# Second expert layer in three 16-bit products on 128-column tiles, its turns taken expert by expert, and the gating as one product a group with a GpSimd addition

## The reference, cut to what matters

```
x = x + windowed_attention(layernorm(x))          # 7x7 windows, 12 heads of 8, shifted by 3 or 4
t = x as tokens
scores = layernorm(t) @ gate_w + gate_b           # 4 experts
probs = softmax(scores);  keep the best 2, divide by their sum
h[e] = gelu(layernorm(t) @ w1[e] + b1[e])         # 96 -> 384, exact gelu
y[e] = h[e] @ w2[e] + b2[e]                       # 384 -> 96: the second expert layer
out = t + sum over e of gate[e] * y[e]
```

## Time and profile before

| | us |
|---|---|
| median of three runs | 7177.02 |
| lowest and highest | 7176.89, 7177.97 |
| the profiled execution | 7177.81 |
| its span, first to last instruction | 7176.0 |
| PE busy | 6927.8 (97%) |
| DVE busy | 5426.9 (76%) |
| ACT busy | 4147.0 (58%) |
| POOL busy | 1515.2 (21%) |
| mean granted TensorE clock | 0.997 of full |

### The profile page before, as it was taken

How to read it: one execution, slowest core, us unless ns; L and a number is a source line. 1 busy time by engine, 2 the same in 40 slices (tenths; PEclk the granted TensorE clock), 3 DMA queues, 4 the chain that set the end, 5 groups by cost and what they waited for, 6 DMA issues and landing times.

```text
span 7176.0 us, 237369 instructions
## 1 busy us (share of the span) xinstructions
PE 6927.8 (97%) x88320; PEld 5767.2 (80%) x88320; DVE 5426.9 (76%) x17442; ACT 4147.0 (58%) x8191; POOL 1515.2 (21%) x777
## 2 busy tenths in 40 slices
PE   5999999999999999999999999999999999999998
PEld 4888788878887888788878887888788878887887
DVE  6777777777777777777777777777777777777775
ACT  3555655565556555655565556555655565556554
POOL 2112211221122112211221122212221222122211
PEclk9999999999999999999999999999999999999999
DMA  1111111111111111111111111111111111111110
GB/s 50 34 35 35 35 34 35 35 35 34 35 35 35 34 35 34 35 34 35 35 35 34 35 34 36 34 35 34 35 34 35 34 36 34 35 34 35 34 34 18
DMA packets 167977, 248.54 MB, mean 35 GB/s; under 512 B 44514, under 2 KB 129122, under 8 KB 166882
## 3 DMA queue, kind: packets, MB, share of 16 engines
q1 hardware_dynamic: 167010, 234.60, 11.7%
...
## 4 chain that ended last, share of the span: by engine, by line
PE 79%; DVE 9%; issue 5%; POOL 4%; ACT 2%; SPq 1%; DVEq 0%; POOLq 0%; DMA 0%
PE ps_f L1041 22%; PE ps_t L953 9%; PE ps_o L970 8%; PE ps_f L881 7%; PE ps_f L883 7%; PE ps_f L882 7%; PE ps_s L933 5%; POOL rstd L412 4%; PE ps_s L943 3%; DVE xr L807 2%; PE ps_f L985 2%; PE ps_t L900 2%; PE ps_f L1038 2%; PE ps_o L979 2%; DVE s_max L669 1%
## 5 line engine op out<-in xcount | busy, mean ns | idle before, releaser
L1041 PE MATMUL ps_f<-w_sb,g_sb 128*112 128x96 f32 x18432 | 1963.0, 261 | 0.0
L1041 PEld LDWEIGHTS ps_f<-w_sb,g_sb 128*112 128x112 f32 x18432 | 1919.6, 178 | 0.0
L502 ACT ACTIVATE pt_sb<-ps_t 113x588 f32<-113x588 f32 x1024 | 677.2, 661 | 1939.0 <-PE ps_t L953 1926.2
L486 ACT ACTIVATE g_sb<-ps_f 128x392 f32<-128x392 f32 x3072 | 1527.5, 497 | 190.3 <-PE ps_f L883 189.4
L412 POOL TENSOR_TENSOR rstd<-ve,cst 112x4 f32<-112x4 f32 (+1 forms) x256 | 269.5, 1053 | 5022.0 <-DVE ve L709 5022.0
L807 DVE SCALAR_TENSOR_TENSOR xr<-ps_f,gate,xr 112x96 f32<-112x96 f32 x3072 | 781.6, 309 | 506.5 <-PE ps_f L1041 506.5
L881 PE MATMUL ps_f<-x_hi,w_hi 128*128 128x392 f16 x3072 | 1012.4, 330 | 97.1 <-DVE x_lo L743 91.1
L883 PE MATMUL ps_f<-x_hi,w_lo 128*128 128x392 f16 x3072 | 1010.8, 329 | 0.0
L882 PE MATMUL ps_f<-x_lo,w_hi 128*128 128x392 f16 x3072 | 1010.7, 329 | 0.0
L669 DVE TENSOR_REDUCE s_max<-ps_s 113x12 f32<-113x588 f32 x1024 | 784.3, 766 | 298.5 <-PE ps_s L943 265.3
L953 PE MATMUL ps_t<-ident,p_sb 113*113 113x113 f32 x6144 | 854.6, 275 | 3.4
...
## 6 DMA issues: line engine op xcount, KB each, us to landing
...
k_st<-qk_lo SPq DMA_DIRECT2D x384, 49.0 KB, 1.9
q_st<-qk_lo SPq DMA_DIRECT2D x384, 49.0 KB, 1.9
...
```

What stands on the lines that cost most here:

```text
L486: nc.scalar.activation(g_sb[:, chunk, half * STRIP:(half + 1) * STRIP], h_bank[k % 3][:, 0:STRIP], ACT.Gelu, scale=1.0 / WSCALE).then_inc( ...
L1041: ins = T.matmul(y[:, k * C:(k + 1) * C], g_sb[:, e * CPE + c, j * LANES:(j + 1) * LANES], w2_sb[:, e * CPE + c, :], start=False, stop=(c ...
```

## The change

The gelu output stays float32 in `g_sb`. For each of its 12 chunks a 16-bit high part is made (`g_hi`, `round_chunk`): of chunks 0 to 5 by DVE, at the start of the step between `spread_keys` and `router_b`; of chunks 6 to 11 by ACT, inside the attention stages (`ROUND_AT`). The remainder is made by GpSimd (`g_lo`, `low_part`, one instruction of 128 x 784 a chunk). Both buffers hold six chunks, so that experts 2 and 3 take the places of 0 and 1. `w2` is split into `w2_hi` and `w2_lo` in the setup, scaled by 64. A turn is now nine 16-bit matmuls in place of three float32 ones, on stationary tiles of 128 columns (16 of them belong to the next tile or to padding). The groups are (expert, 4 tiles) and (expert, 3 tiles), eight in all, of which groups 5, 6 and 7 come after `project`. Gating is one DVE product a group into `y_gated`, and GpSimd adds that to `xr` (`add`).

```diff
-TURNS = [(2 * b + s, e) for b in range(3) for e in range(EXPERTS) for s in range(2)]
-GROUPS_AT = ((0, 1), (2,), (3,), (4,), (), (5,), (6,), ())
-COMBINES_AT = ((0,), (1,), (2,), (3,), (4,), (), (5,), (6,))
+GROUP_TILES = ((0, 4), (4, 3))
+GROUPS_AT = ((0, 1), (2,), (3,), (), (), (4,), (), ())
+COMBINES_AT = ((0,), (1,), (2,), (3,), (), (), (4,), ())
+LATE_GROUPS = (5, 6, 7)
+ROUND_AT = ((), (6, 7), (8,), (), (), (9,), (10, 11), ())
...
+            def low_part(f, chunk):
+                if chunk < 2 * CPE:
+                    pool.wait_ge(hi_dve, at(f, N_ROUND, chunk + 1))
+                else:
+                    pool.wait_ge(hi_act, at(f, N_ROUND, chunk - 2 * CPE + 1))
+                slot = chunk % (2 * CPE)
+                nc.gpsimd.tensor_tensor(g_lo[:, slot, 0:TOK], g_sb[:, chunk, :], g_hi[:, slot, 0:TOK],
+                                        ALU.subtract).then_inc(lo_done, 1)
+            def add(f, u, g):
+                e, j0, n = tiles_of(g)
+                pool.wait_ge(gated, at(f, N_Y, g + 1))
+                if g >= 2:
+                    pool.wait_ge(comb_done, at(f, N_Y, g - 1))
+                slot = xr[:, u, j0 * C:(j0 + n) * C]
+                nc.gpsimd.tensor_tensor(slot, y_gated[:, g % 2, 0:n * C], slot, ALU.add).then_inc(comb_done, 1)
...
             def step(f, a, b, u):  
+                first_half, second_half = range(0, CPE), range(CPE, 2 * CPE)
+                for chunk in first_half:
+                    low_part(f, chunk)
+                for chunk in second_half:
+                    low_part(f, chunk)
+                add(f, u, 0)
+                add(f, u, 1)
                 if b is not None:
                     norm1(b)
+                for chunk in range(2 * CPE, 3 * CPE):
+                    low_part(f, chunk)
+                add(f, u, 2)
+                add(f, u, 3)
+                for chunk in range(3 * CPE, CHUNKS):
+                    low_part(f, chunk)
+                add(f, u, 4)
                 if a is not None:
                     rsqrt2(a)
+                add(f, u, 5)
+                add(f, u, 6)
+                add(f, u, 7)
+                if a is not None:
                     gate_exp(a)
...
             def residual(f, before=None):
                 sums_of(*first_part)
                 variances(*first_part)
+                if before is not None:
+                    combine(before, 5)
                 sums_of(*second_part)
...
                 scale(*second_part)
                 if before is not None:
-                    combine(before, slot_of, 7)
+                    combine(before, 6)
+                    combine(before, 7)
                 x2_low(f, 0)
...
+            def round_chunk(f, chunk):   ; ACT has one of its own
+                dve.wait_ge(gelu_done, at(f, N_H, gelus_of(chunk)))
+                V.tensor_copy(g_hi[:, chunk, 0:TOK], g_sb[:, chunk, :]).then_inc(hi_dve, 1)
+            def combine(f, g):
+                e, j0, n = tiles_of(g)
                 dve.wait_ge(y_done, at(f, N_Y, g + 1))
-                for k, (j, e) in enumerate(TURNS[g]):
-                    V.scalar_tensor_tensor(out=slot, in0=y_bank(g)[0:LANES, k * C:(k + 1) * C],
-                                           scalar=gate[:, j * EXPERTS + e:j * EXPERTS + e + 1], in1=slot,
-                                           op0=ALU.mult, op1=ALU.add).then_inc(comb_done, 1)
+                V.tensor_tensor(y_gated[:, g % 2, 0:n * C].rearrange("p (t c) -> p t c", c=C),
+                                y_bank(g)[0:LANES, 0:n * C].rearrange("p (t c) -> p t c", c=C),
+                                mine.broadcast_to([LANES, n, C]), ALU.mult).then_inc(gated, 1)
...
             def experts(f, g):
+                pe.wait_ge(lo_done, at(f, N_LO, CPE * (e + 1)))
...
-                        ins = T.matmul(y[:, k * C:(k + 1) * C],
-                                       g_sb[:, e * CPE + c, j * LANES:(j + 1) * LANES],
-                                       w2_sb[:, e * CPE + c, :], start=False, stop=(c == CPE - 1),
-                                       skip_group_check=True)
+                        T.matmul(outp, g_hi[:, slot, cols], w2_hi[:, wc], start=False, stop=False,
+                                 skip_group_check=True)
+                        T.matmul(outp, g_hi[:, slot, cols], w2_lo[:, wc], start=False, stop=False,
+                                 skip_group_check=True)
+                        ins = T.matmul(outp, g_lo[:, slot, cols], w2_hi[:, wc], start=False,
+                                       stop=(c == CPE - 1), skip_group_check=True)
```

More of the change, by code:

```diff
@@ L275, in y_bank, with tiles_of, gelus_of @@
             return bank[Y_BANK[g]]
+        def tiles_of(g):
+            return (g // 2, *GROUP_TILES[g % 2])
+        def gelus_of(chunk):
+            return 4 + chunk if chunk < 3 else 2 * chunk + 2
         h_bank = [bank[5], bank[7], bank[6]]
@@ L525, in attention @@
                         exps(a, n + 1)
+                    if f is not None:
+                        for chunk in ROUND_AT[n]:
+                            round_chunk(f, chunk)
                     if n == 4:
@@ L553, in step @@
                     load_tables(ACT.Exp)
-                    attention(a, b)
+                    attention(a, b, f)
+                else:
+                    for chunk in range(2 * CPE, CHUNKS):
+                        round_chunk(f, chunk)
             schedule(act, step, prologue)
@@ L863, in step @@
                     spread_keys(a)
+                for chunk in range(2 * CPE):
+                    round_chunk(f, chunk)
                 router_b(f)
```

132 lines of the change are left out of this document (68 added, 64 removed).

## The result

The kernel after takes 7974.89 us (median of 4 runs, 7973.66 to 7975.47), before 7177.35 us: a ratio of 1.111, 95% interval 1.1097 to 1.1123, slower by 797.5 us or 6.28 us for each of 127 units. Forecast were 8070 us. First the page of the kernel after (as in the earlier trace rows: busy us, share, count), and its chain that ended last.

The account below looks back on a forecast made before the run. PE, busy 97% of the span, was taken to bound the kernel. Path gain -3.4, tail +1.0, lock +6.9 and clock +2.5 sum to +7.0 us a unit, +889 us over 127 units: 8070 us, 8-in-10 range 7600 to 8400.

Parts of the forecast that it names:

- The lock: Start of a step: DVE's two-SBUF-input gate links wait for POOL's six low parts, delaying the first s_max; +6.9 us a unit.
- The product on PE: Expert turns on PE: nine 16-bit matmuls of 96 columns at 0.0425 us each; eight groups 11.8 us against 17.5.
- rival C: Expert matmuls on PE: weight loads come on top, 0.025 us each; +12.4 us a unit, 8750 us, chance 0.05.
- the 392-column row: Trace row of 59 PE matmuls, 0.166 us each with load; taken to price 96 columns at 0.0425 us.
- the line through both rows: Alternative price from PE's 4-column gate matmuls and 392-column matmuls: 0.058 us for 96 columns; not taken.
- The path gain: Attention stages 0, 1, 2, 3, 5 and 6 get shorter by PE's saved work on the path; -3.4 us a unit.
- the tail: End of a unit: later combines on DVE and POOL's add 5 delay x2_lo and the next hidden chunk; +1.0 us a unit.
- The clock: PE idles behind group 0 at the start of a step and returns at the lower clock; +2.5 us a unit (0 to 4).
- The prologue's window: Prologue trace: PE busy 0.33 of 4.10 us, then at 0.57 of its clock; 1.8 us of work lost.
- Rival B: Start of a step: the lock delays, but PE's clock stays at 2.4 GHz; +4.5 us a unit, 7750 us, chance 0.20.
- The later waits: POOL's later work in a unit (norm1, adds, low parts 6 to 11) holds nothing up; cost 0, 4 us of cover.
- Rival A: Start of a step: the lock does not add up, PE never idles; -3.0 us a unit, 6800 us, chance 0.13.

Follow-up runs that it names:

- Run 1: Changed kernel without GpSimd's twelve low parts a unit (g_lo stays zero, all three matmuls still issued); 6944.14 us, 0.967 of before.
- 4: Kernel before with six GpSimd subtractions of 128x784 on scratch tiles added behind gexp; 8022.89 us, 1.1178 of before.
- Run 5: Changed kernel with low parts of chunks 0 to 5 on only columns 0 to 391 of 784; 7209.99 us, 1.0041 of before.
- run 6: Changed kernel with low parts of chunks 6 to 11 left out, those of chunks 0 to 5 kept; 7965.56 us, 1.1095 of before.
- run 11: Kernel before with six GpSimd fills of a 128x784 16-bit tile that read nothing, added behind gexp; 7544.82 us, 1.0509 of before.
- run 2: Changed kernel with the gate chain moved ahead of DVE's six conversions; 7704.79 us, 1.0732 of before.
- run 8: Changed kernel with softmax pairs 0 and 1 ahead of the gate chain on DVE, group 0 behind scores 1 on PE; 7371.49 us.
- run 7: Changed kernel with POOL's add 5 moved between the two powers of the second norm; 7971.62 us, 1.1104 of before.
- run 3: Changed kernel with 30 unused matmuls of 392 columns behind group 0, in PE's idle gap; 7752.73 us, 1.0799 of before.
- run 9: As run 8, but GpSimd's sixth low part waits for the gate; 7419.31 us, 1.0338 of before.

## Why the prediction was right

**The lock, +6.9 forecast, +6.34 measured.** s_max at 18.13 us after the restart against 18.7. Six links are held, as counted, though not the same six: both of the first pair are, and gate is not. Three sizes in it were off, and they partly cancel. The casts are over at 7.70 us, not 8.0; a low part starts every 1.66 us, not every 1.53, so the sixth ends at 17.52 us instead of 17.2. Then the sum put 1.5 us on top, 0.25 for each link, although all but the last of these lie beside the next low part: the chain ends 0.48 us behind the sixth, at 18.0 instead of 18.7. That double counting is the step of the sum that was wrong, and it makes the term 0.6 us too long. Run 1 (no passes, no delay), 4 (passes alone, 4.86 of delay), 5 (shorter pass, shorter link) and 6 (the late six cost 9 us in all) show the cause, and 11 narrows it to passes that read SBUF; runs 2 and 8 show that it is a matter of what stands beside what. The rule of the Trainium skill, "SBUF — State Buffer", "Who interferes with whom", holds in all of them. Its list of operations that lock the shared ports has casts in it, and run 2's casts were locked out (8.87 against 2.94 us). It also says that a DVE instruction with two SBUF inputs does not contend with GpSimd work that only writes; run 11 agrees (0.25 to 0.28 us inside a fill). Its last part, that DVE work with one SBUF input outside the two-port modes is left alone, agrees with run 6 and with rank (0.27 us beside the low parts).

**The product on PE, 0.0425 us a matmul forecast.** 0.0425 measured, at the full clock. Loads that come on top, 0.066 us, are not seen for these 128x128 tiles, and rival C falls with it. The sentence of the Trainium skill's "TensorE: Matmul & The Clock Gate", part 3, "The mechanism", from which the prediction took that rival, does not hold here; the same section also says that a load into the background weight buffer is pulled ahead of matmuls in flight, and that fits 0.0425. The choice of the 392-column row over the line through both rows (0.058) was right.

**The path gain and the tail, -3.4 and +1.0.** Together -2.4 forecast, -2.20 measured in the shown unit, -1.8 in the medians of run 1. The interval from s_max n + 1 to n + 2 is stage n. By the table stage 0 gives 0.56 us (0.6 forecast), stage 1 0.05 (0.18), stage 2 0.63 (0.6), stage 3 0.87 (0.9), stage 5 0.19 (0.18), and the interval of group 0, which the sum left out, 0.18. s_max 7 to gmax is 0.26 longer: if stage 6 gave its 0.9 there, the tail costs 1.16 us, not 1.0; the two were not measured apart. Add 5 holds DVE's scale, 0.96 instead of 0.46 us, as the sum had it, but run 7 gained only 3 us by moving it. The adds themselves were longer than estimated, 1.00 us for 0.75 and 0.79 for 0.56.

**The clock, +2.5 (0 to 4).** 2.09 in the shown unit, 1.75 by run 3. The prologue's window was the right row to go by. Rival B went by the steady state of before, where the longest idle spell is 1.0 us and the clock holds; with the long idle spell of after (5.29 us) it fell in all 127. Run 3, in which the clock holds behind the gap, is B's case and took 7752.73 us, B's 7750, and some of that is luck: its typical unit is 4.15 us longer than before's, not 4.5, and the longer last intervals make up the rest. Shorter spells go either way: in run 8 PE was busy 1.69 of 3.60 us, idle for 1.77 us at a stretch, and the clock was 0.54 in the window behind it; in run 9 it was busy 1.71 of 3.50 us with the same stretch, and the clock stayed at 1.00. What decides between the two is not shown here.

**The later waits, 0.** POOL's six late low parts: 9 us of 7975, run 6.

The sum of the measured terms is 6.34 - 2.20 + 2.09 = 6.23 us, against 7.0 forecast and 6.28 in the medians. Of the 0.8 between them 0.6 is the first term and 0.4 the clock, and the smaller gain takes 0.2 back. Rival A needed less than 2.4 us of delay. Run 5 had 1.9, and its typical unit (54.83 us) is indeed 0.3 us shorter than before's; it came out 0.4% slower all the same, since the clock fell in 31 of its units, 0.4 us a unit in the mean, which A left out, and some starts and last intervals are longer too.

The version that beats both kernels is run 1, 6944 us: it computes two products of three (the third is issued on zeros), at the price of the low part's share of the result.
